# Low-rank output as two float32r products, another order of feed-forward's loop, and transposed x laid out by piece

## What is computed

```python
# part 1: attention with 8 heads of width 8; its projections read x transposed
qk = x @ Wqk_w.T + Wqk_b ;  v = x @ Wv_w.T + Wv_b
...
# part 3: feed-forward with low-rank experts, RANKS = (8, 16, 32, 64), one chosen per token
out = x @ W.T + b
scores = x @ gate_w.T + gate_b
lora = stack([x @ A[:r].T @ B[:, :r].T for r in RANKS])
x = layernorm(x + out + lora[argmax(scores)])
# part 4: projections with 4-bit codes, scales and low-rank parts, then gate/up/down
```

## Time and profile before

| | us |
|---|---|
| median of 3 runs | 645.35 (645.09 to 645.71) |
| the profiled execution | 645.23 |
| its span | 643.1 |
| TensorE busy | 632.0 |
| VectorE busy | 396.3 |
| ScalarE busy | 381.6 |
| feed-forward's loop on TensorE | 131.5 to 191 |

### The profile page before, as it was taken

How to read it: one execution, slowest core, us unless ns; L and a number is a source line. 1 busy time by engine, 2 the same in 40 slices (tenths; PEclk the granted TensorE clock), 3 DMA queues, 4 the chain that set the end, 5 groups by cost and what they waited for, 6 DMA issues and landing times.

```text
span 643.1 us, 8521 instructions
## 1 busy us (share of the span) xinstructions
PE 632.0 (98%) x3226; PEld 470.0 (73%) x3226; DVE 396.3 (62%) x633; ACT 381.6 (59%) x527; POOL 65.0 (10%) x116
## 2 busy tenths in 40 slices
PE   9999999999999999999999999999999999999996
PEld 6655555544558888888888888887777888888874
DVE  4798787667988777767667355335655212125467
ACT  2977789976987697576675154223565343316532
POOL 1032142311330000000000000001211000000012
PEclk9999999999999999999999999999999999999999
DMA  7771585512253134233320003056010322100002
GB/s 246 288 243 52 188 268 172 162 52 92 81 152 120 39 110 139 73 104 111 94 83 2 1 1 131 1 216 274 1 33 2 115 77 88 33 1 0 1 33 99
DMA packets 25590, 63.92 MB, mean 99 GB/s; under 512 B 5541, under 2 KB 10725, under 8 KB 24782
## 3 DMA queue, kind: packets, MB, share of 16 engines
q1 hardware_dynamic: 23294, 61.68, 29.4%
q10 hardware_dynamic: 2256, 1.70, 0.8%
HBM read 58.77 MB, written 4.60 MB: 99 GB/s over the span
## 4 chain that ended last, share of the span: by engine, by line
PE 88%; DVE 4%; ACT 4%; DMA 1%; issue 1%; SPq 1%; POOL 0%; POOLq 0%; DVEq 0%; ACTq 0%
PE bank L1043 18%; PE bank L1031 8%; PE bank L1030 8%; PE bank L1032 8%; PE bank L1122 8%; PE bank L1121 8%; PE bank L882 4%; PE bank L802 3%; PE bank L606 3%; PE bank L741 2%; PE bank L1097 1%; DMA codes<-in_c_qkv 1%; PE bank L912 1%; PE bank L926 1%; PE bank L984 1%
## 5 line engine op out<-in xcount | busy, mean ns | idle before, releaser
L1232 ACT ACTIVATE line<-line 128x1024 f32<-128x1024 f32 x87 | 91.4, 1050 | 0.2
L1030 PE MATMUL bank<-xh,wh 128*128 128x512 f32 x224 | 87.5, 391 | 0.0
L1031 PE MATMUL bank<-xl,wh 128*128 128x512 f32 x224 | 87.5, 391 | 0.0
L1032 PE MATMUL bank<-xh,wl 128*128 128x512 f32 x224 | 87.3, 390 | 0.0
L1043 PE MATMUL bank<-wh,xh 128*128 128x512 f32 x192 | 76.1, 396 | 0.2 <-DVE xl L2128 0.2
L1043 PE MATMUL bank<-wh,xl 128*128 128x512 f32 x192 | 74.9, 390 | 0.0
L2211 DVE SCALAR_TENSOR_TENSOR arena<-bank,ff_s,arena 128x512 f32<-128x512 f32 x28 | 21.0, 752 | 72.9 <-PE bank L1122 63.8
L2128 DVE TENSOR_TENSOR xl<-arena,xh 128x1024 fp32r<-128x1024 f32 (+1 forms) x26 | 29.7, 1141 | 35.4 <-ACT xh L1536 35.3
L1121 PE MATMUL bank<-xh,wh 128*128 128x512 f32 x128 | 50.3, 393 | 0.0
L1536 ACT ACTIVATE xh<-arena 128x1024 fp32r<-128x1024 f32 (+1 forms) x26 | 25.6, 991 | 41.3 <-PE bank L1043 34.8
L1122 PE MATMUL bank<-xl,wh 128*128 128x512 f32 x128 | 49.9, 390 | 0.0
(11 more groups left out here) (219 smaller groups left out, 1264.3 us busy)
## 6 DMA issues: line engine op xcount, KB each, us to landing
codes<-in_c_gu SPq DMA_DIRECT2D x14, 512.0 KB, 3.8
scales<-in_s_gu SPq DMA_DIRECT2D x28, 256.0 KB, 4.0
codes<-in_t_gu SPq DMA_DIRECT2D x8, 512.0 KB, 4.2
codes<-in_c_dn SPq DMA_DIRECT2D x7, 512.0 KB, 4.6
scales<-in_s_dn SPq DMA_DIRECT2D x14, 256.0 KB, 3.9
fold<-in_t_dn SPq DMA_DIRECT2D x1, 3584.0 KB, 15.7
codes<-in_c_qkv SPq DMA_DIRECT2D x6, 512.0 KB, 4.8
scales<-in_t_gu SPq DMA_DIRECT2D x6, 512.0 KB, 3.8
```

The lines of the kernel that those rows point to most:

```text
L1030: pe.matmul(dst, wh[:, s, c:c + P], xh[:, k, cols], start=(k == 0), stop=False)
L1031: pe.matmul(dst, wh[:, s, c:c + P], xl[:, k, cols], start=False, stop=False)
L1032: last = pe.matmul(dst, wl[:, s, c:c + P], xh[:, k, cols], start=False, stop=(k == KD - 1))
L1232: nc.scalar.activation(below(slot), below(slot), ACT.Prelu, bias=bias, scale=scale, alpha=alpha).then_inc(bent, 1)
```

## The change

- The low-rank output becomes two float32r products. `choose` writes the chosen values rounded (`lm_high`, columns 64 to 127) and their rest (columns 0 to 63, in place) side by side; `lora_T` transposes all 128 columns; `lora_T_out` writes `lm_both` (128 rows) and `lm_one` (the high rows again, and two rows of ones); `lora_out` multiplies `lm_both` by `b_both` and 97 rows of `lm_one` by `b_high_one`. These two are made once, by `experts_high` on ScalarE and `experts_low` on VectorE, from two loads (256 and 194 KB) that take the place of one of 130 KB and are issued later.
- ScalarE's loop: `lora_T_out(t + 1)` and `x_T_out` stand ahead of the second half of the bends; `lora_T_out(t)` stood at the start.
- VectorE's loop: `ln_head(t)` stands ahead of `choose(t + 2)`; `x_low` of block t - 2 stands at the end of t, ahead of the second half of the units; it stood at the start of t + 1.
- Transposed x comes from DRAM in piece order, each piece's row one stretch of 4 KB. Piece 0 is cut by slices (two of four) instead of tokens, so `qk_projection(0)` is 4 products of 256 columns. ScalarE waits for piece 0's first half before it asks for pieces 1 and 2.

```diff
+        with nc.sbuf_tensor("lm_one", [P, T], F32R) as lm_one:
+            pass
         folded_m = sb("folded", [P, T])
...
-        lmT = sb("lmT", [P, 2, P])
-        probT = lmT
+        with nc.sbuf_tensor("lm_both", [P, 2, P], F32R) as lm_both:
+            pass
+        probT = sb("probT", [P, 2, P])
...
+        x_piece = [xT[:, KD * n * PC:KD * (n + 1) * PC] for n in range(NP)]
+        x_part = [m.rearrange("p (j c) -> p j c", j=KD) for m in x_piece]
...
+        b_low_at = at
         bT0, at = carve(arena, at, D)
...
+        b_high_at = at
         wk2, at = carve(arena, at, D)
...
-        lm, w_at = carve(early_w, w_at, 2 * RMAX)
-        assert w_at <= 2 * CH
+        lm = early_w[:, FF:2 * CH]
+        assert w_at <= 2 * CH and 2 * CH - FF == 4 * RMAX and 2 * RMAX == P
+        lm_high = wl[:, :, :].rearrange("p s c -> p (s c)")[:, FF:2 * CH].rearrange("p (s c) -> p s c", s=2)
...
+        b_two, b_one = wk3, m_free[:, 0:D]
+        b_both, b_high_one = arena_r[:, b_low_at:b_low_at + D], arena_r[:, b_high_at:b_high_at + D]
+        ONE_ROWS = slice(RMAX, RMAX + ROWG + 1)
+        lm_one = lm_one[:, 0:2 * P].rearrange("p (s t) -> p s t", s=2)
...
-                sp.dma_start(xT[:, :, n * PC:(n + 1) * PC], i["xT"][:, :, n * PC:(n + 1) * PC]).then_inc(in_x[n], 16)
+                sp.dma_start(x_piece[n], i["xT"][:, n, :]).then_inc(in_x[n], 16)
...
@@ -533,7 +545,6 @@
             keys_out(0)
             sp.wait_ge(kw_ps, KD + 2)
             sp.dma_start(w0T, i["w0T"]).then_inc(in_ffn0, 16)
-            sp.dma_start(bT0[0:RMAX + 1, :], i["bT0"]).then_inc(in_ffn0, 16)
             load_scales(C_O)
             keys_out(1)
             load_codes(C_O + 1)
...
                     load_codes(C_O + 1 + t // 2)
+                if t == KD:
+                    sp.dma_start(b_two, i["b_two"]).then_inc(in_ffn0, 16)
+                    sp.dma_start(b_one[0:ONE_ROWS.stop, :], i["b_one"]).then_inc(in_ffn0, 16)
...
                     pe.wait_ge(qk_ready, (0, 0, 1, 3)[n])
-                for h in range(2) if n == 0 else (0,):
-                    size = P if n == 0 else PC
-                    if h:
+                for k in range(KD):
+                    if n == 0 and k == KD // 2:
                         pe.wait_ge(in_x0b, 16)
-                    t = slice(n * PC + h * P, n * PC + h * P + size)
-                    for k in range(KD):
-                        last = pe.matmul(bank[QK_BANK[n]][:, h * P:h * P + size], qkT[:, k, :], xT[:, k, t], start=(k == 0), stop=(k == KD - 1))
+                    last = pe.matmul(bank[QK_BANK[n]][:, 0:PC], qkT[:, k, :], x_part[n][:, k, :], start=(k == 0), stop=(k == KD - 1))
                 last.then_inc(qk_ps, 1)
...
-                    pe.wait_ge(in_ffn0, 48)
+                    pe.wait_ge(in_ffn0, 64)
                     pe.wait_ge(kq_ready, NT - 1)
                 elif b == 1:
                     pe.wait_ge(kq_ready, NT)
@@ -883,11 +894,14 @@
             def lora_T(b):
                 pe.wait_ge(lm_ready, b + 1)
-                pe.transpose(turn_bank(b)[0:RMAX, P:2 * P], lm[:, b % 2, :], ident[:, :]).then_inc(lm_ps, 1)
+                pe.transpose(turn_bank(b)[:, P:2 * P], lm[:, b % 2, :], ident[:, :]).then_inc(lm_ps, 1)
             def lora_out(b):
                 pe.wait_ge(lmT_ready, b + 1)
-                pe.matmul(bank[FF_BANK[b % 3]][:, :], lmT[0:RMAX + 1, b % 2, :], bT0[0:RMAX + 1, :], start=False, stop=True).then_inc(f0_ps, 1)
+                if b == 0:
+                    pe.wait_ge(lm_ready, 2)
+                pe.matmul(bank[FF_BANK[b % 3]][:, :], lm_both[:, b % 2, :], b_both, start=False, stop=False)
+                pe.matmul(bank[FF_BANK[b % 3]][:, :], lm_one[0:ONE_ROWS.stop, b % 2, :], b_high_one[0:ONE_ROWS.stop, :], start=False, stop=True).then_inc(f0_ps, 1)
             def attention_lora(n):
...
-            def piece_in(n, size):
-                nc.scalar.dma_start(xT[:, :, n * PC:n * PC + size], i["xT"][:, :, n * PC:n * PC + size]).then_inc(in_x[n], 16)
-
-            piece_in(0, P)
-            nc.scalar.dma_start(xT[:, :, P:PC], i["xT"][:, :, P:PC]).then_inc(in_x0b, 16)
-            piece_in(1, PC)
-            piece_in(2, PC)
+            half = KD * PC // 2
+            nc.scalar.dma_start(x_piece[0][:, 0:half], i["xT"][:, 0, 0:half]).then_inc(in_x[0], 16)
+            nc.scalar.dma_start(x_piece[0][:, half:], i["xT"][:, 0, half:]).then_inc(in_x0b, 16)
+            act.wait_ge(in_x[0], 16)
+            for n in (1, 2):
+                nc.scalar.dma_start(x_piece[n], i["xT"][:, n, :]).then_inc(in_x[n], 16)
             act.wait_ge(blank, 1)
             nc.scalar.activation(small[0:1, 1, 31:32], mz_flat[0:1, 0:1], ACT.Identity)
             rows_out_of(0)
...
+            def experts_high():
+
+                act.wait_ge(in_ffn0, 64)
+                nc.scalar.activation(b_both, b_two, ACT.Copy)
+                nc.scalar.activation(b_high_one[0:ONE_ROWS.stop, :], b_one[0:ONE_ROWS.stop, :], ACT.Copy).then_inc(stack_hi, 1)
+
             for t in range(1, NT + 2):
+                if t == NT + 1:
+                    experts_high()
                 if 2 <= t < NT:
                     sims_exp(t)
                 for u, h in half_plan(2, t, 0):
...
-                nc.scalar.activation(lmT[0:RMAX, b % 2, :], turn_bank(b)[0:RMAX, P:2 * P], ACT.Copy).then_inc(lmT_ready, 1)
-
+                nc.scalar.activation(lm_both[:, b % 2, :], turn_bank(b)[:, P:2 * P], ACT.Copy)
+                nc.scalar.activation(lm_one[0:RMAX, b % 2, :], turn_bank(b)[RMAX:P, P:2 * P], ACT.Copy).then_inc(lmT_ready, 1)
+
+            act.wait_ge(kb_out, 16 * KD)
+            for n in range(2):
+                nc.scalar.activation(lm_one[ONE_ROWS, n, :], ident[ONE_ROWS, :], ACT.Identity, bias=1.0, scale=0.0)
+
+            lora_T_out(0)
             for t in range(NT):
-                lora_T_out(t)
                 for u, h in half_plan(3, t, 0):
                     unit_bends(u, h)
                 if t >= 1:
                     norm_tail(2 * NT + t - 1)
                 if FIRST_M <= t < FIRST_M + KD:
                     m_high_of(t - FIRST_M)
-                for u, h in half_plan(3, t, 1):
-                    unit_bends(u, h)
-                if t == 1:
+                if t == 2:
                     for n in range(2):
                         act.wait_ge(kq_out[n], 16 * NT // 2)
                 if t >= 2:
                     x_T_out(2 * NT + t - 2, dst=xh)
+                if t + 1 < NT:
+                    lora_T_out(t + 1)
+                for u, h in half_plan(3, t, 1):
+                    unit_bends(u, h)
                 if t < 2:
                     stack_hi_of(t)
                 elif t < 4:
...
-            nc.vector.memset(lmT[RMAX:RMAX + 1, :, :], 1.0)
             nc.vector.memset(wb[:, 2 * KD:2 * KD + 1], 0.0)
             nc.vector.memset(ones[:, :], 1.0)
...
-                nc.vector.tensor_tensor(lm[:, s, :].rearrange("p (r m) -> p r m", m=SEG), ps[:, 0:RMAX].rearrange("p (r m) -> p r m", m=SEG),
-                                        mask.unsqueeze(1).to_broadcast([P, RMAX // SEG, SEG]), ALU.mult).then_inc(lm_ready, 1)
+                chosen, high = lm[:, s, 0:RMAX], lm_high[:, s, RMAX:P]
+                link(nc.vector.tensor_tensor(chosen.rearrange("p (r m) -> p r m", m=SEG), ps[:, 0:RMAX].rearrange("p (r m) -> p r m", m=SEG),
+                                             mask.unsqueeze(1).to_broadcast([P, RMAX // SEG, SEG]), ALU.mult))
+                link(nc.vector.tensor_copy(high, chosen))
+                nc.vector.tensor_tensor(chosen, chosen, f32(high), ALU.subtract).then_inc(lm_ready, 1)
+
+            def experts_low():
+
+                dve.wait_ge(stack_hi, 1)
+                low, row = slice(RMAX, P), slice(RMAX + ROWG, RMAX + ROWG + 1)
+                nc.vector.tensor_tensor(b_both[low, :], b_two[low, :], f32(b_both[low, :]), ALU.subtract)
+                nc.vector.tensor_tensor(b_high_one[row, :], b_one[row, :], f32(b_high_one[row, :]), ALU.subtract)
             def add_lora(n):
...
-                dve.wait_ge(stack_hi, part + 1)
+                dve.wait_ge(stack_hi, 1 + part + 1)
                 if part == 0:
                     nc.vector.tensor_tensor(a_st[2 * RG:STACK, :], a_gu[2 * RG:STACK, :], f32(a_st[2 * RG:STACK, :]), ALU.subtract).then_inc(stack_low, 1)
                 else:
...
+            experts_low()
             choose(1)
             dve.wait_ge(kq_ps, NT)
             for t in range(NT):
-                if t >= 3:
-                    x_low(2 * NT + t - 3)
                 for n in range(AF0 * t, min(AF0 * (t + 1), 2 * KD)):
                     add_lora(n)
                 if t in (1, 2):
@@ -2020,14 +2056,15 @@
                     unit_part(u, h)
                 if t == 4:
                     down_stack_low()
+                dve.wait_ge(f0_ps, t + 1)
+                ln_head(2 * NT + t, plus(FF_BANK[t % 3]))
                 if t + 2 < NT:
                     choose(t + 2)
```

(16 more changed lines are left out.)

## The result

The changed kernel takes 647.92 us (median, 647.40 to 648.85); the kernel before, run beside it, 645.42. The ratio is 1.0045 [1.0035, 1.0056], slower by 0.45%; the two medians are 2.50 us apart. I had put 0.50 on "within 0.2%", at 646.3, and 0.37 on slower; 647.92 is at the upper edge of my range, 643.6 to 648.0, but inside it. The profiled execution took 647.40 with a span of 645.6 us.

The account below looks back on a forecast made before the run. The prediction took TensorE and VectorE to be at their limit together in feed-forward's loop. From 645.23 us, +1.2 for the loop and -0.2 for the start gave 646.2, as a median 646.3, range 643.6 to 648.0.

Parts of the forecast that it names:

- What bounds it: Feed-forward's loop, 131 to 191 us: TensorE and VectorE both at their limit, VectorE's queue without holes.
- The terms for TensorE: Low-rank output: two float32r products hold the queue 0.47 us instead of 0.88, saving 0.41 a block, 3.3 in all.
- The terms for VectorE: `choose`: linked multiply, added copy (0.16 long) and subtraction cost +0.44 us a block, bounds 0.28 and 0.50.
- The walk: Feed-forward's loop, new order laid over old durations: `attention_product(0)` about 156.8, `x_T(2, 4)` 183.64, loop end +1.2 us.
- The hole: TensorE's wait ahead of `x_T(2, 4)`, there at about 181.0 but held until 183.64: some 2.5 us.
- the sum: Whole kernel: 645.23 + 1.2 for the loop - 0.2 for the start = 646.2; as a median 646.3 us.
- The step that failed: Behind `x_T(2, 4)`: `lora_T(7)` and `ffn_W(7)` end at 187.6, then `attention_out(0)` starts at 188.1.
- The start: Transposed x and first product: at best 0.77 us less, ScalarE ready at about 7.5; -0.2 (from -0.6 to +0.5).
- A: Rival for the loop: TensorE stays the bound, -3.3 us and the start's -0.2, 641.9, half of it 643.6; chance 0.13.
- C: Rival: nothing moves, added steps cost their lower bound, +0.2 in the loop, -0.2 at the start, 645.3; chance 0.15.
- B: Rival: VectorE's and ScalarE's queues interlock, `m_high(3)` after 187.3 delays `attention_out(0)`; 647.3, or 647.7; chance 0.22.

Follow-up runs that it names:

- e10: The changed kernel with two more linked 128x64 copies in VectorE's `choose` for blocks 2 to 7; 651.23 us, ratio 1.0099.
- e7: The changed kernel with `choose`'s copy and subtraction moved from VectorE to GpSimd; 644.67 us, ratio 0.9993.
- e9: e7 with five steps of ScalarE and VectorE moved earlier, for TensorE's three remaining waits; 643.91 us, ratio 0.9977.
- e4: The changed kernel with three float32 products that nobody reads put into TensorE's two waits near 181 and 183; 646.65 us, ratio 1.0019.
- e6: The changed kernel without `choose`'s copy and subtraction for blocks 2 to 7, so outputs are not the reference's; 645.44 us, ratio 0.9997.
- e5: The changed kernel with `ffn_W(7)` put ahead of `x_T(2, 4)` on TensorE; 647.07 us, ratio 1.0031.
- e1: The changed kernel with ScalarE's and VectorE's loops put back into the order of before; 648.96 us, ratio 1.0053.
- e3: The kernel before with only the changed kernel's transposed x and its loads, feed-forward as before; 645.37 us, ratio 1.0008.

## Why the prediction went wrong

**What bounds it.** Right. VectorE's queue is the limit up to `x_T(2, 4)`: e10 gives 2.73 us for 2.76 added. With VectorE relieved (e7, e9), 0.88 and 2.18 us of TensorE's saving arrive.

**The terms for TensorE.** Nearly right. The two float32r products hold the queue 0.47 us in block 7 (192.32 to 192.79), as forecast, but 0.54 to 0.56 in blocks 0 to 5 (137.10 to 137.65 in block 0). There the product ahead of them, `ranks`, gives up its place 0.07 earlier (0.81 us after its start, 0.88 before), so that either way a block saves 0.39 us, for the 0.41 forecast, and eight save 3.1.

**The terms for VectorE.** Right. Its timeline for the last four steps of `choose(2)` and what follows:

```profile
139.84 0.17 DVE L1989 TENSOR_TENSOR gate_v<-gate_v 128x8 f32<-128x8 f32 x1
140.05 0.23 DVE L1993 TENSOR_TENSOR early_w<-bank,gate_v 128x64 f32<-128x64 f32 x1
140.31 0.20 DVE L1995 CAST wl<-early_w 128x64 fp32r<-128x64 f32 x1
140.54 0.23 DVE L1996 TENSOR_TENSOR early_w<-early_w,wl 128x64 f32<-128x64 f32 x1
140.68 1.22 DVE L1785 SCALAR_TENSOR_TENSOR fold<-line,scales 128x1024 f32<-128x1024 f32 x1
```

From the start of the multiply to the next work are 0.63 us, 0.14 before: +0.49 by this pair of rows, of which the copy is 0.20 where I had 0.16; over a whole `choose` I read 1.28 against 0.82 to 0.87 before, +0.41 to +0.46, around the 0.44 forecast. The trace decides against the estimate of 0.13 for the copy that I worked out from the table in the Trainium skill ("VectorE: DVE Perf Modes", section on the TRN2 errata).

**The walk.** Right to a few tenths, hole by hole. `ln_head(0)` was to start at 137.81 and starts at 137.85; `attention_product(0)` at about 156.8, 156.86; VectorE's resumption at 162.0, 162.18; `x_T(2, 4)` at 183.64, 183.83. The hole was to be 2.5 us and is 2.2, in two parts: I had `lmT`'s successor for block 6 ready in time, but `lora_out(6)` waits 0.57 for `lm_one`. Both hang on the same queues, and `x_T(2, 4)` swallows it. The wait ahead of `attention_product(0)` is 0.32 for some 0.5, and TensorE had lost 0.58 and 0.45 before it, at `ffn_W(4)` and `ffn_W(5)`; the walk had named only the second of these. These rows of VectorE carry the walk:

```profile
137.85 0.69 DVE L1832 TENSOR_TENSOR rbuf<-x,bank 128x512 f32<-128x512 f32 x1 [1.19 <-PE bank L904]
...
162.18 0.69 DVE L1832 TENSOR_TENSOR rbuf<-x,bank 128x512 f32<-128x512 f32 x1 [2.91 <-PE bank L904]
...
187.41 0.66 DVE L2035 SCALAR_TENSOR_TENSOR arena_r<-bank,m_hi 128x512 fp32r<-128x512 f32 x1
```

With the clock kept (e4), `x_T(2, 5)` starts 68.66 us behind `ffn_W(0)`, 1.27 later than before (67.39), for the +1.2 that the sum carries.

**The step that failed** is the one behind the hole: "`lora_T(7)` and `ffn_W(7)` end at 187.6." I took the durations of the trace of before, 3.44 us for the product, as if a wait cost only its own length. They hold at a granted clock of 1.00. The hole took the clock down to 0.50, and from `x_T(2, 4)` to the next stage TensorE needed 5.86 us (183.83 to 189.69) where it had needed 4.18 (182.54 to 186.72). Of these 1.68 us, 0.4 would have gone anyway into the wait for `m_low(3)`, which was done at 188.07 (e4, with the clock kept, needs 0.38 more than before on this way); 1.3 are net. A term for the clock was missing from the sum. With it the forecast would have been 647.6, and 647.8 without the 0.2 that the start did not bring. I had named a hole of 2.5 us on an engine with a gated clock and not asked what the clock would do.
The Trainium skill ("TensorE: Matmul & The Clock Gate", Part 1) says of the gate that the throttled state is the default and that activity releases it; the rows from 183 to 188 agree (0.50 from 184 to 187 us, behind the waits), and so does e4, which adds only activity in the waits and keeps 1.00.

**The start.** Forecast -0.2 (from -0.6 to +0.5), measured nothing (`ffn_W(0)` starts at 122.83, 122.82 before), and for another reason than mine. I had ScalarE limit it at 7.5 us. ScalarE waits for TensorE instead:

```profile
1.08 3.78 PE L628 MATMUL bank<-fold 128*128 128x256 f32 x8 [1.08 <-POOL fold L1711]
4.65 2.79 PE L640 MATMUL bank<-arena,early_w 128*128 128x256 f32 x8
```

```profile
7.54 0.47 ACT L1316 ACTIVATE project<-bank,qk_b 128x256 f32<-128x256 f32 x1 [0.81 <-PE bank L640]
```

The 8 products of 256 columns take 2.79 us, not the 1.89 of the same form later on the earlier trace rows. The warm-up products ahead of them, of the same size, take 3.78: in this execution the records run at half pace from the engine's first work until about 6.4 us. I had taken the price from a row at full pace. Piece 1 was in time (9.96, before 10.00), as forecast.

The pace is not the whole answer, since it differs between executions (the same 8 products take 1.89 us in e4's and 3.01 in e6's). In e4's they have the price that I gave them, and TensorE is 0.9 us ahead at 26.41, where it was at 27.34 before. Yet `ffn_W(0)` starts at 122.69, only 0.13 earlier. In between ScalarE waits longer for a transfer of codes, 1.12 us for 0.33, and TensorE then 1.18 us for ScalarE's exponentials, for 0.38:

```profile
26.04 1.06 ACT L1247 ACTIVATE line<-codes 128x1024 f32<-128x1024 int32 x1 [1.12 <-DMA codes<-in_c_qkv]
```

```profile
32.64 0.73 PE L690 MATMUL bank<-heads 9*128 9x128 f32 x16 [1.18 <-ACT fold L1343]
```

So even at the price that I had put down, the gain is given back at 33 us in this execution. My walk of the start ended at 10 us and did not see that.

**The rivals.** A (TensorE stays the bound) is refuted: it needed TensorE's waits to go or VectorE's work to be 2 us shorter, and there are five waits, with VectorE where I had it. C (nothing moves) fell with the added steps, which cost what they were to cost. B named a size, 647.3 to 647.7, that is nearly the one measured, for a cause that did not occur. Its mechanism was `m_high(3)` after 187.3 for want of codes: it is done at 186.7 (starts 186.11, 0.60 long). That the measured time fits B's number is an accident, and so is its lying in my range, whose upper part was there for B.

What stays open: which waits lower the clock and which don't. In the changed kernel 0.57 and 1.60 us, close together, did, and in e10 a single one of 2.95. In e5 0.58 and 1.92, with 4.7 us of work between them, did not. But neither did 1.21 and 1.28 in e1, with 0.8 us of work between them, and these look no milder than the first. The product at 33 us says the same: it waits 1.17 us in e1, 1.08 in e10 and 2.24 in e3, and the clock falls behind it (0.50 to 0.54 from 36 to 38 us); it waits 1.18 in e4, and the clock stays. So a rule can't be read from these rows. Each kernel has one profiled execution (that of the changed kernel is the shortest of its six); that the medians of after and e4 differ by 1.27 us, as the profiled lengths do (1.30), speaks for the fall in most executions of after, but they were not looked at one by one. e1's higher median may be the same clock in others of its executions; that is not shown.

## What to carry to other kernels

When you forecast that an engine with a gated clock gets a hole, the hole may not be the whole price: ask whether the clock can fall behind it, and give that a term of its own, with the next work priced from rows at the lower clock. These runs don't say which holes do it, so it is a chance and not a certainty. A saving on the engine that is 98% busy was worth nothing here while a second queue without holes fed it. Count what the edit adds there, one for one, and look for a third engine with room: here GpSimd took the same two steps at no cost in time, and the kernel went from 1.0045 to 0.9993 of the time before, which can't be told from 1. Then look at the waits that come next: e9's five moved steps brought 0.9977. And two variants of equal length need not have lost it in the same way: e1 and the changed kernel have 73.07 and 73.20, one by waits alone, the other by waits and a lower clock.

## What was not expected of the hardware

- The granted clock can fall behind waits that are together only 2.2 us long: 0.50 in the windows from 184 to 187 us, behind 0.57 and 1.60. And it can stay up behind 1.21 and 1.28 (e1). At the lower clock eight products of 512 columns took 4.87 us, for 3.60 to 3.70.
- At the start the profile's granted clock reads 1.00 in every window, while records of 256 columns are 634 ns long (379 to 634 in the first real product) until 6.4 us in the changed kernel's execution, and in e4's only until 4.7. There the price of a product is read from the pace of the records, not from the column.
- GpSimd did the 128x64 cast in 0.23 us and the subtraction in 0.32, against 0.20 and 0.23 on VectorE, whose own steps did not get longer beside it (the multiply at 179.51 is 0.22, `x_low` 0.68).
